# Two global attentions recomputed in groups of 32 partitions, with a pipeline over eight tasks

## Time and profile before

| | us |
|---|---|
| median of 3 runs (lowest to highest) | 8913.92 (8912.63 to 8922.38) |
| the profiled execution | 8909.57 |
| its span, first to last instruction | 8907.7 |
| before the first statistics of x | 0 to 12.3 |
| the two global attentions, 4 batch entries | 12.3 to 925.7 |
| attention over the batch | 925.7 to 1071 |
| ODE stage, preparation and loop | 1071 to 7683 |
| rest of it, window attention, experts | 7683 to 8907.7 |

### The profile page before, as it was taken

The page is one execution under the profiler, slowest core; times in us unless marked ns, Lnnn a source line. Parts: engine busy times, 40 slices in busy tenths (PEclk is TensorE's granted clock), DMA queues, the critical chain, the costliest instruction groups (busy, mean ns, idle before and its releaser), DMA issues. The chain is left out here.

```text
span 8907.7 us, 387903 instructions
## 1 busy us (share of the span) xinstructions
PE 8128.0 (91%) x148885; PEld 5201.3 (58%) x148885; DVE 5894.3 (66%) x33160; ACT 2874.7 (32%) x10559; POOL 1260.6 (14%) x5288
## 2 busy tenths in 40 slices
PE   7777499999999999999999999999999999755886
PEld 3333166666666666666666666666666666544675
DVE  5665466666666666666666666666666666545997
ACT  4444122222222222222222222222222222235886
POOL 1000011111111111111111111111111111101001
PEclk9888599999999999999999999999999999867887
DMA  3110000000000000000000000000000000002332
GB/s 118 57 64 39 25 4 4 4 4 4 4 4 4 4 4 4 4 4 4 4 4 4 4 4 4 4 4 4 4 4 4 4 4 4 4 0 90 120 126 84
DMA packets 39897, 185.38 MB, mean 21 GB/s; under 512 B 7108, under 2 KB 20999, under 8 KB 27927
## 3 DMA queue, kind: packets, MB, share of 16 engines
q1 hardware_dynamic: 25638, 92.62, 2.7%
q0 software_dynamic: 12400, 67.68, 2.0%
HBM read 122.66 MB, written 37.62 MB: 18 GB/s over the span
## 5 line engine op out<-in xcount | busy, mean ns | idle before, releaser
L594 PEld LDWEIGHTS p<-H,W 128*128 128x128 f16 x130816 | 3572.9, 96 | 1940.8 <-DVE H L745 1918.8
L594 PE MATMUL p<-H,W 128*128 128x8 f16 x130816 | 3942.4, 167 | 74.7 <-DVE H L745 62.5
L606 PE MATMUL p<-W 128*128 128x500 f16 x12264 | 3261.0, 374 | 0.0
L745 DVE SCALAR_TENSOR_TENSOR H<-h,H 128x8 f16<-128x8 f32 x10220 | 1503.1, 163 | 279.7
L680 ACT ACTIVATE h<-u 128x8 f32<-128x8 f32 x4088 | 853.0, 209 | 2436.5 <-DVE u L765 2281.3
L675 ACT ACTIVATE h<-r 128x8 f32<-128x8 f32 x4088 | 851.7, 209 | 2405.0 <-DVE r L773 2220.5
L765 DVE TENSOR_REDUCE u<-p 128x8 f32<-128x24 f32 x6132 | 964.7, 175 | 804.2 <-PE p L594 804.2
L773 DVE TENSOR_REDUCE r<-p 128x8 f32<-128x24 f32 x4088 | 746.3, 183 | 1054.5 <-PE p L594 813.8
L740 DVE TENSOR_SCALAR H<-h 128x8 f16<-128x8 f32 x8176 | 1396.3, 171 | 41.0 <-issue 26.4
L606 PEld LDWEIGHTS p<-W 128*128 128x128 f16 x12264 | 884.1, 96 | 474.3 <-issue 9.4
L570 POOL TENSOR_TENSOR twice<-r 128x16 f32<-128x16 f32 x511 | 110.1, 215 | 2865.7 <-DVE r L773 2865.7
(11 more groups left out here) (328 smaller groups left out, 4939.2 us busy)
## 6 DMA issues: line engine op xcount, KB each, us to landing
e_W<-w_scaled SPq DMA_DIRECT2D x23, 2304.0 KB, 10.0
e_W<-w_scaled SPq DMA_DIRECT2D x23, 1152.0 KB, 5.1
raw<-in_spline POOLq DMA_DIRECT2D x24, 1024.0 KB, 6.8
w_scaled<-raw POOLq DMA_DIRECT2D x8, 2304.0 KB, 7.9
w_scaled<-raw POOLq DMA_DIRECT2D x8, 1152.0 KB, 10.0
raw<-in_base POOLq DMA_DIRECT2D x24, 128.0 KB, 6.6
raw_s<-in_scaler POOLq DMA_DIRECT2D x24, 128.0 KB, 7.0
rows_in<-zeros POOLq DMA_DIRECT2D x4, 768.0 KB, 16.3
```

What stands on the lines that cost most here:

```text
L594: ins = pe.matmul(out[:, m, 0:2 * B], W[:, q, k, P * m:P * m + P], H[:, k, :, :].rearrange("p q b -> p (q b)"), start=fresh[m], stop=(left ...
L606: pe.matmul(out[:, k, 3 * B:S], W2[:, 0, k, 0:P], W2[:, 1, k, 3 * B:S], start=True, stop=True, skip_group_check=True)
L745: sg.up(dve.scalar_tensor_tensor(out=Hq[:, :, 1, :], in0=mb(cols(h, q)), scalar=HSCALE, in1=Hq[:, :, 0, :], op0=ALU.mult, op1=ALU.subtract ...
```

## The change

**Row groups.** The four pairs of heads lie in four groups of 32 partitions; head 2g+p is the half p of group g. A score is now a matmul over the 32 partitions of its group (`by_query`, `by_key`), with the other half zeroed in `qm`. A unit is (p, tile j, group g), with g running fastest.

**Scores twice.** `by_query` makes a score tile with queries on the partitions, and only its row maximum is taken. Four transposes for each task turn all maxima, and `shift_queries` writes them into the free half of the queries, while the keys carry a 1 there. `by_key` then makes the same scores, shifted by their maximum, with keys on the partitions, so that exp gives the transposed weights directly. The transposes, the copy after them and the multiplication by 1/sum for each unit are gone.

**Column groups.** `weigh` multiplies 32 columns of `vhat` (16 values and a column of ones, which gives the sum) into the group's 32 partitions of `pO`, four matmuls for each tile of keys. The division by the sum comes once for each task (`finish`).

**Pipeline.** The loop over b is gone. The tasks n = 0 to 7 are layer 0 of the four entries, then layer 1. In round n PE interleaves `by_query` of task n, `by_key` and `weigh` of task n-1, and `finish` of task n-2; ten rounds in all. The group norm and first layer norm of all four entries come before round 0. The last layer norms run in rounds 8 and 9 and after them.

**Expert weights.** Expert 7 is scaled in round 8. The others are scaled in the ODE loop: in evaluation 1 of steps 4 to 55 of each round DVE does half of an instruction's columns, and SP loads and stores.

```diff
+    UNITS, TASKS = HEADS * QT, 2 * B
+    GROUPS = 4
...
+        qm, khat, qhat, osb = pair("qm"), pair("khat", 3), pair("qhat"), pair("osb")
+        vhat = [sb(f"vhat{k}", [P, QT, 2, GROUPS, 32]) for k in range(3)]
+        nmq = [sb(f"nmq{k}", [P, QT, P]) for k in range(2)]
+        PT = [sb(f"PT{k}", [P, S]) for k in range(8)]
...
+        pA, pC = [ps(f"pA{n}") for n in range(3)], [ps(f"pC{n}") for n in range(3)]
+        pO, pM = ps("pO"), ps("pM")
...
+            raw.load(pool, a, NE - 1, sg, "ew_load")
...
+            def by_query(n, u):
+                p, j, g = u // 16, u // 4 % 4, u % 4
+                rows = slice(32 * g, 32 * g + 32)
+                if u == 0:
+                    sg.wait(pe, "khat", 2 * n + 2)
+                if n or u >= 3:
+                    sg.wait(pe, "a_max", UNITS * n + u - 2)
+                sg.up(pe.matmul(pA[(UNITS * n + u) % 3][:], qm[n % 2][p][rows, j * P:(j + 1) * P], khat[n % 3][p][rows, :],
+                                start=True, stop=True), "a_ps")
+
+            def by_key(n, u):
+                p, j, g = u // 16, u // 4 % 4, u % 4
+                rows = slice(32 * g, 32 * g + 32)
+                if u == 0:
+                    sg.wait(pe, "qhat", 2 * n + 2)
+                if n or u >= 3:
+                    sg.wait(pe, "prob", UNITS * n + u - 2)
+                sg.up(pe.matmul(pC[(UNITS * n + u) % 3][:], khat[n % 3][p][rows, j * P:(j + 1) * P], qhat[n % 2][p][rows, :],
+                                start=True, stop=True), "c_ps")
+
+            def weigh(n, k):
+                p, j = k // 4, k % 4
+                sg.wait(pe, "prob", UNITS * n + 4 * k + 4)
+                if k == 0:
+                    sg.wait(pe, "vhat", 2 * n + 2)
+                if j == 0:
+                    sg.wait(pe, "o_copy", 2 * n + p)
+                for g in range(GROUPS):
+                    ins = pe.matmul(pO[32 * g:32 * g + 32, :], vhat[n % 3][:, j, p, g, :], PT[(4 * k + g) % 8][:], start=(j == 0), stop=(j == 3))
+                sg.up(ins, "pv")
+
+            def maxima_turned(n):
+                sg.wait(pe, "a_max", UNITS * n + UNITS)
+                if n + 1 < TASKS:
+                    sg.wait(pe, "vhat", 2 * n + 4)
+                elif n >= 2:
+                    sg.wait(pe, "x2_done", batch(n - 2) + 1)
+                for j in range(QT):
+                    ins = pe.transpose(pM[:, j * P:(j + 1) * P], nmq[n % 2][:, j, :], t.ident[:])
+                sg.up(ins, "nm_ps")
...
+            for n in range(TASKS + 2):
+                for u in range(UNITS):
+                    if n >= 2:
+                        finish(n - 2, u)
+                    if n < TASKS:
+                        by_query(n, u)
+                    if 1 <= n <= TASKS:
+                        by_key(n - 1, u)
+                        if u % 4 == 3 and u > 4:
+                            weigh(n - 1, u // 4 - 1)
+                    if n + 1 < TASKS:
+                        if u == 23:
+                            queries(n + 1)
+                        elif u == 26:
+                            keys(n + 1)
+                        elif u == 29:
+                            values(n + 1)
+                    if n == TASKS and u in (3, 4):
+                        z_mean(u - 3, pA[u - 3])
+                    if n == TASKS and u in (11, 12):
+                        if u == 12:
+                            sg.wait(pe, "n3_cent", 2)
+                        z_var(u - 11, (pA[2], pA[0])[u - 11])
+                if 1 <= n <= TASKS:
+                    weigh(n - 1, 7)
+                if n < TASKS:
+                    maxima_turned(n)
...
+            def prob(n, u):
+                sg.wait(act, "c_ps", UNITS * n + u + 1)
+                sg.wait(act, "pv", 8 * n + u // 4 - 1)
+                sg.up(act.activation(PT[u % 8][:], pC[(UNITS * n + u) % 3][:], ACT.Exp), "prob")
+
+            def copy_o(n, p):
+                sg.wait(act, "pv", 8 * n + 4 * p + 4)
+                if n >= 2:
+                    sg.wait(act, "o_ps", n - 1)
+                sg.up(act.activation(osb[n % 2][p][:], pO[:], ACT.Copy), "o_copy")
...
+            def maximum(n, u):
+                p, j, g = u // 16, u // 4 % 4, u % 4
+                at = 32 * g + 16 * (1 - p)
+                sg.wait(dve, "a_ps", UNITS * n + u + 1)
+                if n >= 2 and u == 0:
+                    sg.wait(dve, "nm_ps", n - 1)
+                sg.up(dve.tensor_reduce(nmq[n % 2][:, j, at:at + 1], pA[(UNITS * n + u) % 3][:], AX.X, ALU.max, negate=True), "a_max")
+
+            def shift_queries(n, p):
+                sg.wait(dve, "nm_ps", n + 1)
+                if n >= 2:
+                    sg.wait(dve, "c_ps", UNITS * (n - 1))
+                sg.up(dve.scalar_tensor_tensor(out=qhat[n % 2][p][:], in0=pM[:], scalar=mask(1 - p), in1=qm[n % 2][p][:],
+                                               op0=ALU.mult, op1=ALU.add), "qhat")
+
+            def finish(n, u):
+                l, b = layer(n), batch(n)
+                if u == 3:
+                    sg.wait(dve, "sum_ps", n + 1)
+                    if n:
+                        sg.wait(dve, "o_norm", n)
+                    sg.up(dve.reciprocal(rr[:], pM[:]), "r_done")
+                elif u == 8:
+                    sg.wait(dve, "o_ps", n + 1)
+                    sg.wait(dve, "r_done", n + 1)
+                    sg.up(dve.tensor_tensor(oT[:], pM[:], rr[:], ALU.mult), "o_norm")
...
+                    if n == TASKS and u >= 22:
+                        if u == 22:
+                            sg.wait(dve, "ew_load", 16 * ExpertWeights.LOADS)
+                        for k in range(3 * (u - 22), min(3 * (u - 22) + 3, ExpertWeights.PARTS)):
+                            ins = raw.scale(dve, k)
+                        if u == 30:
+                            sg.up(ins, "ew_scaled")
...
+            for e in range(STEPS // UN):
+                raw.load(sp, t.dram, e, sg, "ew_load")
+                sg.wait(sp, "ew_scaled", e + 1)
+                raw.store(sp, t, e, sg, "ew_store")
+                sg.wait(sp, "ew_store", 16 * ExpertWeights.STORES * (e + 1))
...
+                        if e == 1 and 4 <= w < 4 + 2 * ExpertWeights.PARTS:
+                            if w == 4:
+                                dve.wait_ge(sg.sem["ew_load"], i * (16 * ExpertWeights.LOADS) + 16 * ExpertWeights.LOADS)
+                            ins = raw.scale_half(dve, (w - 4) // 2, w % 2)
+                            if w == 3 + 2 * ExpertWeights.PARTS:
+                                sg.up(ins, "ew_scaled")
...
+    def scale_half(self, dve, n, k):
+        first, second = self.first, self.second
+        if n < 2 * NB:
+            x = first[:, n % 2, n // 2, C * k:C * k + C]
+            return dve.tensor_tensor(x, x, self.s12[:, n % 2, C * k:C * k + C], ALU.mult)
+        if n < 3 * NB:
+            x = second[:, k, n - 2 * NB, :]
+            return dve.tensor_tensor(x, x, self.s3[:, k, :], ALU.mult)
+        x = (first if n == 3 * NB else second)[:, k, NB, :]
```

More of the change, by code:

```diff
@@ new lines, in _ @@
+            for b in range(B):
+                sg.wait(pe, "g_dev2", b + 1)
+                sg.up(pe.matmul(banks[4 + b][:, 0:1], g4[:], dev[:, b:b + 1], start=True, stop=True), "g_var_ps")
+            for b in range(B):
+                sg.wait(pe, "gx", b + 1)
+                sg.up(pe.matmul(banks[b][:], t.ones[:], gx[b][:], start=True, stop=True), "n1_mean")
+            for b in range(B):
+                sg.wait(pe, "n1_sq", b + 1)
+                sg.up(pe.matmul(banks[4 + b][:], t.ones[:], sq[b][:], start=True, stop=True), "n1_var")
@@ new lines, in _, with queries @@
+            sg.wait(pe, "preset", 11)
+            def queries(n):
+                x, wq, _, _, ready = project(n)
+                sg.wait(pe, ready, batch(n) + 1)
+                if n == 0:
+                    sg.wait(pe, "n1_sd", B)
+                else:
+                    sg.wait(pe, "qhat", 2 * n - 2)
+                    if n >= 3:
+                        sg.wait(pe, "x1_part" if layer(n - 3) == 0 else "x2_done", batch(n - 3) + 1)
+                if layer(n):
+                    pe.matmul(pM[:], w1qe[:], emb[:], start=True, stop=False)
+                sg.up(pe.matmul(pM[:], wq, x[:], start=not layer(n), stop=True), "q_ps")
@@ new lines, in keys, with values @@
+            def keys(n):
+                x, _, wk, _, _ = project(n)
+                sg.wait(pe, "qm", 2 * n + 2)
+                if layer(n):
+                    pe.matmul(pM[:], w1ke[:], emb[:], start=True, stop=False)
+                sg.up(pe.matmul(pM[:], wk, x[:], start=not layer(n), stop=True), "k_ps")
+            def values(n):
+                x, _, _, wv, _ = project(n)
+                sg.wait(pe, "khat", 2 * n + 2)
+                for j in range(QT):
+                    o = pM[:, j * C:(j + 1) * C]
+                    ins = pe.matmul(o, x[:, j * P:(j + 1) * P], wv, start=True, stop=bool(layer(n)))
```

(22 more changed lines are left out.)

437 lines of the change are left out of this document (233 added, 204 removed).

## The result

The changed kernel takes 8697.66 us (median of 4 runs, 8677.69 to 8719.51) against 8914.99 for before in the same rounds: a ratio of 0.9755, 95% interval 0.973 to 0.9781, 217 us less. The forecast was 8630, 284 less. The profiled execution took 8689.44, its span 8687.6.

The account below looks back on a forecast made before the run. PE bounds the attention units, before and after; the stage falls from 925.7 to 642 us, 284 less, the ODE loop adds 0, so 8909.6 - 284 = 8625.6, plus 4 for the median: 8630 us. Range 8375 to 9000.

Parts of the forecast that it names:

- Which work bounds the kernel before: Attention units before: PE bounds them, with 2.3 of 2.58 us a unit; DVE has 1.7 us in each.
- The scaling in the ODE loop: 364 added DVE products of 0.29 us hide in evaluation 1's wait for PE: cost 0, without cover 106 us.
- PE's overlap: Scores and weighing in the units: neighbouring groups overlap by half, so four units take 7.26 us, 7.5 at most.
- C(g): Score by key of row group g, said to wait for its own group's score by query; a pair costs 1.28 us.
- A(g+1): Score by query of the next row group, said to start beside the second half of the preceding score by key.
- The reciprocal of 3.35: DVE's reciprocal in a task: it holds up maxima, three banks deep, but costs nothing at 1.8 us a unit.
- Rival 3: Unused rows count as rest, the clock stays at 1.2 GHz: round 139 us, stage 235 longer, 9150 us; chance 0.19.
- 56% of the rounds: Share of rounds at the low clock from which its loss outweighs the 284 us gain: 284 / (7 x 68 + 34).
- The forecast's stage of 642: Global attentions: 49 + 28 + 497 + 41 + 27 = 642 us against 925.7, 284 us less.
- round 8 and the end: Round 8, score by key and weighing without new queries' scores, 41 us; last finish and layer norms 27 us.
- the 58.5 and 7.3 of the forecast: PE time for units: 58.5 us a task at 1.83 a unit; 7.26 us for four units before size changes.
- 71 us a round: Each of rounds 1 to 7: 58.5 for units, 9.6 other PE work and 3 of new waits.

Follow-up runs that it names:

- moved: Kernel before, with only the scaling of experts 0 to 6 put in the ODE loop and its attentions otherwise kept: 8928.5 us, ratio 1.0012.
- probe: TensorE alone, no kernel work: streams of float32 matmuls on row or column groups without waits; four row groups in turn 0.22 us each, one alone 0.87 at full clock.
- blocks: Only the changed kernel's four-unit block, repeated: changed order, all rows, rotated order 4.81, 8.05, 3.96 us a block; with an added DVE wait 6.87, 8.64, 6.64.
- cheap: Changed kernel with the twelve 128x512 reciprocals inside the rounds replaced by a multiply and add writing a constant: 8582.73 us, ratio 0.9629 to before.
- rot: Changed kernel with by_key taking row groups in the order 2, 3, 0, 1, the rotated order: 8557.24 us, ratio 0.9593 to before.
- fill2: Changed kernel with two float16 filler matmuls over all rows and columns ahead of each block of four units: 8688.4 us, ratio 0.9741 to before.

## Why the prediction was right or wrong

**Which work bounds the kernel before: supported.** moved took 208 products from DVE, and its attentions became only 16 us shorter. The scaling in the ODE loop costs nothing that the traces can tell, as forecast: 6559 us in the changed kernel, 6569 before, with 0.25 us of waiting left in evaluation 1. Only moved itself has 6595, for an unknown reason.

**PE's overlap: wrong.** The failed step is "C(g) waits for its own row group, A(g+1) can start beside the second half of C(g). So a pair costs three half times". Row groups work off their matmuls independently: three or four run at once, in probe at exactly a fourth of the price, and in the kernel a block costs 4.81 us at full clock, not 7.26. What limits it is the fourth unit, which waits for a bank, as the timeline shows and the rotated order confirms (3.96 us a block in blocks).

**"The reciprocal of 3.35 holds up maxima, three banks deep, so at 1.8 us a unit it costs nothing": wrong.** Without them the time is 115 us less. What PE waits for in the trace is not the maxima but the result itself, 7.7 us in six waits. That the rest of the 115 comes through the clock fits the windows of cheap, but no run holds the clock and takes the reciprocals away.

**The clock: the right suspicion under a wrong condition.** Rival 3 took unused rows for rest and let the clock be low throughout. It is low for part of the time (0.68). One row group alone did lose it in probe, but in blocks neither the changed order without a pause nor a pause over all rows did. A mean of 0.68 means the low level for (1 - 0.68) / 0.5 = 64% of the time, more than the 56% of the rounds from which I had the change slower; it stays faster because a block costs less than I had counted at the high level (4.81 for 7.3) and at the low one 8.4 to 9.3, not twice 7.3.

**The sizes.** The forecast's stage of 642 became 712.9: to the first maximum 46.1 for 49, round 0 35.9 for 28 (PE busy for 33 of it at a clock of 0.55, where I took DVE as the bound), rounds 1 to 7 535.4 for 497, round 8 and the end 95.6 for 68 (clock 0.61 to 680 us). That is -3 + 8 + 38 + 28 = 71 us short of the gain; the ODE loop is 10 us shorter, about what it differs from kernel to kernel (6557 to 6573).

In a round the units are not the term that is short. Of the 535.4 us of rounds 1 to 7, PE is busy for 493.5. Projections, transposes and `finish` take 119.5 of them, 17.1 a round where I had 9.6, counted at full clock. PE waits for 41.9, 6.0 a round where I had 3. That leaves 374 for the units, 53.4 a round or 6.7 us a block, less than the 58.5 and 7.3 of the forecast. So the mis-sized terms are the other work and the waits. The 6.7 is a mean of blocks of 4.8 and of 8.4 to 9.3: two wrong steps, an overlap too small and a clock too high, nearly cancelled in it. That 71 us a round came out near 76.5 was luck to that extent, and so was the range.

**What beats both.** rot, at 8557, is the fastest kernel here that computes the reference: 1.6% below the changed one by the medians.

## What to carry to other kernels

Matmuls on 32 of the 128 rows ran side by side at their full share (0.22 us each for 0.87), even in the order g, g, g+1, g+1, so order them such that a matmul that must wait for a bank doesn't leave its group alone in the array. Then count what the speed costs: at half the length, waits for other engines that were covered come into the open, and in blocks a pause of half a microsecond in a block of five cost two, because the clock fell. Judge such a change by the granted clock and the length of the same block at different places; an array that looks busy may be running at half speed. And look at a run that "changed nothing" stage by stage: moved and fill2 each hide a gain and a loss of 16 to 26 us behind a total that stood still.

## What the hardware showed that was not expected

- One group of 32 rows without any pause: 24 matmuls in 36.7 us at a clock of 0.56; 64 rows, or 32 columns, in 20.8 to 20.9 at 1.00.
- Four row groups in turn without a pause, and all rows with a pause of 0.52 us a block, kept 1.00; row groups with a pause came to 0.71 and 0.78 (blocks).
- A float32 reciprocal of 128x128 on DVE took 0.94 us where one of 128x512 took 3.35: four quarters cost 0.4 more than the whole.
